# Query and key stacks of the attention layer: two heads by TensorE, six by 64 KB transfers, and one ring for the transposed weights

## The reference

```python
q, k, v = proj(Wq, bq), proj(Wk, bk), proj(Wv, bv)      # 8 heads of 32
scores = einsum('bhqd,bhkd->bhqk', q, k) * SCALE
scores = scores * (adj + adj)[:, None, :, :]
attn = softmax(scores, axis=-1)
ctx = einsum('bhqk,bhkd->bhqd', attn, v)
out = ctx @ Wo.T + bo
```

## Time and profile before

| | |
|---|---|
| median of three runs | 3148.42 us (3145.5 to 3149.03) |
| profiled execution | 3147.59 us |
| its span, first to last instruction | 3145.7 us |
| PE busy | 3023.7 us, 96% |
| DVE busy | 2083.8 us, 66% |
| ACT busy | 1724.0 us, 55% |
| POOL busy | 453.5 us, 14% |
| mean granted TensorE clock | 0.993 of full speed |
| DMA moved | 234.50 MB, mean 75 GB/s |

### The profile page before, as it was taken

How to read it: one execution, slowest core, us unless ns; L and a number is a source line. 1 busy time by engine, 2 the same in 40 slices (tenths; PEclk the granted TensorE clock), 3 DMA queues, 4 the chain that set the end, 5 groups by cost and what they waited for, 6 DMA issues and landing times.

```text
span 3145.7 us, 71077 instructions
## 1 busy us (share of the span) xinstructions
PE 3023.7 (96%) x28188; PEld 2644.0 (84%) x28188; DVE 2083.8 (66%) x4020; ACT 1724.0 (55%) x3048; POOL 453.5 (14%) x1666
## 2 busy tenths in 40 slices
PE   6999999999999999999999999999999999999999
PEld 6988789887898778987789877898778987789877
DVE  5637976379762797627975289753887438874387
ACT  3525854258552684426844278542784327853377
POOL 0101211012110122101221012111121111211112
PEclk9999999999999999999999999999999999999999
DMA  5122131121321213202133021330213302133110
GB/s 218 36 72 69 45 145 54 57 70 45 142 77 37 66 52 135 90 28 66 49 135 108 11 72 42 135 108 14 68 51 125 108 14 72 50 124 108 28 39 19
DMA packets 145271, 234.50 MB, mean 75 GB/s; under 512 B 12840, under 2 KB 113965, under 8 KB 144941
## 3 DMA queue, kind: packets, MB, share of 16 engines
q1 hardware_dynamic: 144940, 229.96, 22.5%
HBM read 120.86 MB, written 83.89 MB: 65 GB/s over the span
## 4 chain that ended last, share of the span: by engine, by line
PE 80%; DVE 10%; ACT 3%; issue 2%; SPq 2%; POOL 2%; DMA 0%; DVEq 0%; POOLq 0%; ACTq 0%
PE ps L725 15%; PE ps L497 15%; PE ps L499 14%; PE ps L498 14%; PE ps L715 9%; PE ps L743 7%; DVE rsum L1280 2%; PE ps L598 2%; SPq L400 1%; PE ps L587 1%; PE ps L756 1%; DVE ev L1379 1%; PE ps L555 1%; DVE t_lo L1210 1%; POOL rstd L461 1%
## 5 line engine op out<-in xcount | busy, mean ns | idle before, releaser
L1466 DVE CUSTOM_DVE_ANT_0 r<-ps,adjn 128x1024 f32<-128x1024 f32 x512 | 620.7, 1212 | 19.5 <-DVE xr L1502 10.3
L1141 ACT ACTIVATE r<-r,nmax 128x1024 f32<-128x1024 f32 x512 | 584.9, 1142 | 23.0 <-POOL nmax L489 22.6
L497 PE MATMUL ps<-u_hi,t_hi 128*128 128x256 f32 x2048 | 589.9, 288 | 5.8 <-DVE u_lo L1190 4.8
L499 PE MATMUL ps<-u_hi,t_lo 128*128 128x256 f32 x2048 | 579.2, 283 | 0.0
L498 PE MATMUL ps<-u_lo,t_hi 128*128 128x256 f32 x2048 | 578.8, 283 | 0.0
L725 PEld LDWEIGHTS ps<-ident,r 128*128 128x128 f32 x4096 | 462.5, 141 | 115.4 <-issue 77.6
L725 PE MATMUL ps<-ident,r 128*128 128x128 f32 x4096 | 536.7, 274 | 7.3 <-DVE pt L1482 6.9
L1482 DVE COPY pt<-ps 128x512 f32<-128x512 f32 x512 | 352.9, 689 | 92.6 <-PE ps L725 75.0
L497 PEld LDWEIGHTS ps<-u_hi,t_hi 128*128 128x128 f32 x2048 | 391.2, 191 | 14.3 <-DVE t_lo L1190 7.7
L907 ACT ACTIVATE pt<-ps 128x512 f32<-128x512 f32 x512 | 304.0, 594 | 175.8 <-PE ps L725 161.9
L498 PEld LDWEIGHTS ps<-u_lo,t_hi 128*128 128x128 f32 x2048 | 391.1, 191 | 0.0
(11 more groups left out here) (162 smaller groups left out, 5233.9 us busy)
## 6 DMA issues: line engine op xcount, KB each, us to landing
adjn<-in_adj SPq DMA_DIRECT2D x64, 512.0 KB, 3.4
t_spill<-t_hi SPq DMA_DIRECT2D x64, 512.0 KB, 4.5
t_spill<-t_lo SPq DMA_DIRECT2D x64, 512.0 KB, 5.3
t_hi<-t_spill SPq DMA_DIRECT2D x32, 1024.0 KB, 5.3
t_lo<-t_spill SPq DMA_DIRECT2D x32, 1024.0 KB, 8.0
xn<-in_x SPq DMA_DIRECT2D x16, 512.0 KB, 4.5
x_spill<-xn SPq DMA_DIRECT2D x64, 128.0 KB, 1.7
q_stack<-u_hi SPq DMA_DIRECT2D x64, 128.0 KB, 2.4
```

Of the source, the lines that this page charges most:

```text
L497: pe.matmul(dst, a_hi, b_hi, start=first, stop=False, skip_group_check=check)
L499: return pe.matmul(dst, a_lo, b_hi, start=False, stop=last, skip_group_check=check)
L1141: act.activation(r[:, s % RSLOTS, :], r[:, s % RSLOTS, :], ACT.Exp, bias=nmax[:, s % 4:s % 4 + 1], accum_out=prow[:, qt % 2, h:h + 1]).the ...
L1466: dve.tensor_tensor_reduce(out=r[:, s % RSLOTS, :], in0=ps[:, 2 * (s % 2):2 * (s % 2) + 2, :].rearrange("p a c -> p (a c)"), in1=adjn[:, q ...
```

## The change

Only heads 0 and 1 are placed by PE (`PLACED = 2`), and only their first query half and both key halves: six copies instead of 16. Everything else comes by DMA in transfers of 32 rows x 512 columns, 64 KB: for heads 2 to 7 both first halves (36) and the second key halves (18), and the second query halves of all eight heads (24), which are needed from unit 32 on. That is 78 transfers for 24. Parts are projected in another order, the first halves first, so that SP can begin when the second of the eight parts is complete; part 7 is projected behind the scores of unit 0.

The transposed weights get one ring of 15 slots for both halves, in an order that reuses the memory of the projections as their transfers complete. The single wait for all transfers becomes several: DVE and ACT wait for the first halves of heads 4 to 7 at unit 0, DVE for their second key halves at unit 2, and both for the second query halves at halves 11 to 14 of the ring, which are units 5 to 7. DVE also waits before it masks units 0 and 1, for heads 2 and 3.

```diff
-    COPIES = [(h, m, half) for half in range(HALVES) for m in range(2) for h in range(G)]
+    PLACED = 2
+    COPIES = [(h, m, half) for m, half in ((1, 0), (0, 0), (1, 1)) for h in range(PLACED)]
-    QK = [(1, 0, 0), (1, 1, 0), (0, 0, 0), (0, 1, 0), (1, 0, 1), (1, 1, 1), (0, 0, 1), (0, 1, 1)]
+    QK = [(0, 1, 0), (0, 0, 0), (1, 1, 0), (1, 0, 0), (0, 1, 1), (1, 1, 1), (0, 0, 1), (1, 0, 1)]
+        P_RING = ([(pt_0, k) for k in (2, 0, 6, 4, 3)] + [(pt_1, k) for k in range(6)] +
+                  [(pt_0, 1), (pt_0, 5), (pt_2, 0), (pt_2, 1)])
         def p_half(u, half):
+            tile, k = P_RING[(2 * u + half) % PSLOTS]
+            return tile[:, k, :, :]
...
-                for g in range(G):                       # SP: 24 transfers, 128 KB each
-                    ...
+                def moved(h, m, half, signal):           # three transfers, 64 KB each
+                    src_rows, at = slice(HD * (h % G), HD * (h % G + 1)), slice(half * 512, (half + 1) * 512)
+                    stack = (q_stack, k_stack)[m]
+                    for part, lo in enumerate((0, 0, 1) if m == 0 else (1, 0, 0)):
+                        sp.dma_start(f32(stack[HD * part:HD * (part + 1), h, at]),
+                                     f32(qk_place((h // G, m, half), lo)[src_rows, :])).then_inc(signal, 16)
+                part_done((0, 0, 0))
+                first_halves(range(PLACED, G))           # 12 transfers
+                part_done((1, 0, 0))
+                first_halves(range(G, G + 1))            # 6
+                part_done((0, 1, 1))
+                key_halves(range(PLACED, G))             # 6
+                first_halves(range(G + 1, H))            # 18
+                part_done((1, 1, 1))
+                key_halves(range(G, H))                  # 12
+                part_done((1, 0, 1))
+                for g in (1, 0):
+                    for h in range(G * g, G * (g + 1)):
+                        moved(h, 0, 1, queries_in[g])    # 24
+                wait_keys(sp, b, range(G, H))
...
+                        if u == 0:                       # ACT, before it copies half 1 of unit u
+                            wait_first(act, b, range(G, H))
+                        if 2 * u + 1 == 11:
+                            wait_queries(act, b, 1)
+                        if 2 * u + 1 == 13:
+                            wait_queries(act, b, 0)
-                        if u >= P1SLOTS:
-                            act.wait_ge(ctx_done, nth(b, 2 * NT, (u - P1SLOTS) // G + 1))
+                        if u >= 7:
+                            act.wait_ge(ctx_half, nth(b, 2 * NT, (u - 7) // G + 1))
...
+                        if u == 0:                       # DVE, before it copies half 0 of unit u
+                            wait_first(dve, b, range(G, H))
+                        if u == 2:
+                            wait_keys(dve, b, range(G, H))
+                        if 2 * u == 12:
+                            wait_queries(dve, b, 1)
+                        if 2 * u == 14:
+                            wait_queries(dve, b, 0)
```

More of the change, by code:

```diff
@@ L251, in build_program @@
         qk_hi = sem("qk_hi")
-        stacked = [sem(f"stacked{g}") for g in range(G)]
+        first_in = [sem(f"first_in{h}") for h in range(PLACED, H)]
+        keys_in = [sem(f"keys_in{h}") for h in range(PLACED, H)]
+        queries_in = [sem(f"queries_in{g}") for g in range(2)]
         copies_full = sem("copies_full")
@@ L281, in nth, with qk_place, wait_first, wait_keys @@
             return b * per + n
-        def qk_place(part, staged, kept):
+        def qk_place(part, lo):
             ft, m, half = part
-            return (staged[:, m * N + half * 512:m * N + (half + 1) * 512] if ft == 1 else
-                    kept[:, m, half * 512:(half + 1) * 512])
+            if ft == 1:
+                return (u_lo if lo else u_hi)[:, m * N + half * 512:m * N + (half + 1) * 512]
+            at = N + lo * N + half * 512 if m == 1 else 3 * N * half + lo * 512
+            return qk0[:, at:at + 512]
+        def wait_first(eng, b, heads):
+            for h in heads:
+                eng.wait_ge(first_in[h - PLACED], nth(b, 16 * 6, 16 * 6))
+        def wait_keys(eng, b, heads):
+            for h in heads:
+                eng.wait_ge(keys_in[h - PLACED], nth(b, 16 * 3, 16 * 3))
+        def wait_queries(eng, b, g):
+            eng.wait_ge(queries_in[g], nth(b, 16 * 3 * G, 16 * 3 * G))
         def copies_place(n):
@@ L388, in element @@
                     sp.dma_start(x3_d[t], xn[:, t, :]).then_inc(spilled[t // TPH], 16)
-                for g in range(G):
[L392 to L400, removed]
@@ new lines, in first_halves, with key_halves @@
+                def first_halves(heads):
+                    for h in heads:
+                        for m in range(2):
+                            moved(h, m, 0, first_in[h - PLACED])
+                def key_halves(heads):
+                    for h in heads:
+                        moved(h, 1, 1, keys_in[h - PLACED])
+                part_done = lambda part: sp.wait_ge(pr_free, nth(b, PR_UNITS, pr["qk", part] + 1))
+                part_done((0, 0, 0))
+                first_halves(range(PLACED, G))
@@ L689, in stack_copies @@
                 pe.wait_ge(pr_free, nth(b, PR_UNITS, pr["qk", (0, m, half)] + 1))
-                if 4 <= n < 3 * G or n >= 3 * G + 2:
-                    copied(b, n - (4 if n < 3 * G else 2))
-                at = slice(half * 512, (half + 1) * 512)
+                hi, lo = qk_place((0, m, half), 0), qk_place((0, m, half), 1)
                 block = lambda k, count: placer[:, (4 * h + k) * HD:(4 * h + k + count) * HD]
@@ L864, in _, with qk_part @@
                         transpose_x_half(b, 3, 0)
[L867 to L874, removed]
+                def qk_part(n):
+                    ft, m, half = QK[n]
                     pe.wait_ge(tp_free, nth(b, TP_UNITS, x_ready(3, TPH * half + TPH - 1)))
@@ L881, in _ @@
                     last.then_inc(pr_full, 1)
-                for n in range(G, 3 * G + 2):
+                qk_part(0)
+                transpose_x_late(b, 3, 1)
+                qk_part(1)
+                transpose_x_late(b, 3, 2)
+                qk_part(2)
+                qk_part(3)
+                project_pairs(b, "values", W_V, xt_wait(b, 3), range(1))
+                qk_part(4)
+                for n in range(2 * PLACED):
                     stack_copies(b, n)
+                qk_part(5)
+                for n in range(2 * PLACED, 3 * PLACED):
+                    stack_copies(b, n)
+                qk_part(6)
                 scores(b, 0)
+                qk_part(7)
                 for s in range(UNITS + 10):
```

97 lines of the change are left out of this document (49 added, 48 removed).

## The result

The changed kernel takes 3290.6 us (median of 4 runs, 3287.6 to 3293.2) against 3148.7 for the kernel before: 1.045 of its time, 95% interval 1.0438 to 1.0463. It is slower, by 142 us. The profiled execution took 3287.58 us, its span is 3285.8, its mean granted clock 0.971.

The account below looks back on a forecast made before the run. PE was taken to bound the kernel before, and SP's 78 issues to hold up the changed one. Eight elements of 16.6 + 1.5 - 0.1 us give 144 us on 3147.6: 3290 us predicted, range 3195 to 3325.

Parts of the forecast that it names:

- PE's share: Before the first scores: fewer placement matmuls bring the first mask 5.3 us earlier an element, 42 us over eight.
- The price of an issue: SP's stack transfers: 64 KB costs 0.655 us an issue, as 128 KB does; below 0.44 us the change would be faster.
- the general argument behind it: SP's other issues: 128 KB has 0.320 us, 1 MB 0.360, so half the bytes would not halve the price.
- The waits: ACT and DVE copies in units 0 to 7: transfers land late, holding the whole loop 16.6 us an element.
- unit 2's copy: DVE's copy at unit 2, awaiting the 54th transfer: at 686.9 where it stood at 677.99, 8.9 us late.
- half 1 of unit 6: ACT's copy there, awaiting the 78th transfer: at 702.6 where it stood at 685.95, 16.6 us late.
- ends just in time: Kernel before: its stream of 24 stack transfers was read as ending just in time for the ACT and DVE copies.
- The clock: After PE's idle wait: a lower granted clock costs nothing at best, 5 us at worst; 1.5 us an element taken.
- The sum: Eight elements of delay 16.6 plus clock 1.5 less 0.1 us: 144 us on 3147.6, said as 3290 us.
- The lower end of the range: The sum's own low end, 3250 us: 0.60 us an issue, no clock loss, 13 us an element.
- the cheap issue: Rival on SP's burst: 64 KB takes 0.32 to 0.37 us an issue, nobody waits, 3105 us; chance 14%.
- the in-between one: Rival on SP's burst: 0.47 to 0.60 us an issue; at 0.535, 7.3 us late, 3206 us; chance 17%.

Follow-up runs that it names:

- v3: The changed kernel with its 78 stack transfers shared by two issuing engines, 42 on SP and 36 on GpSimd: 3117.8 us, ratio 0.9905.
- x1: The changed kernel with its 42 query transfers of an element cut from 64 KB to 16 KB, keys as before: 3288.0 us, ratio 1.0448.
- x2: The kernel before with each of its 24 stack transfers of 128 KB cut in two of 64 KB: 3271.4 us, ratio 1.0402.
- x4: The changed kernel with query transfers of 128 rows x 128 columns instead of 32 rows x 512, again 64 KB: 3295.4 us, ratio 1.0471.
- x5: The changed kernel with query transfers of 32 rows x 256 columns (32 KB) read from DRAM and not from SBUF: 3236.1 us, ratio 1.0273.
- x7: The kernel before with both query parts of heads 4 to 7 complete at the fourth part and queries moved before keys: 3146.1 us, ratio 0.9987.
- x6: The changed kernel with 48 matmuls into a free part of a bank before PE waits for unit 7's second copy: 3277.8 us, ratio 1.0407.
- x8: The changed kernel with the 24 second query halves issued by GpSimd, SP keeping 54 transfers: 3221.7 us, ratio 1.0233.
- v1: The changed kernel with projections sent through DRAM in 16 stores and 21 loads, 37 issues for 78: 3165.5 us, ratio 1.0051.

## Why the prediction was right

**PE's share**: first mask 661.9, predicted 662.1. In all eight elements it comes 5.5 us earlier, for 5.3 predicted, and v3 keeps 4.1 of them.

**The price of an issue**: 0.655 us, taken from the row of the same shape. The eight bursts last 50.6 to 51.6 us, mean 50.95 / 78 = 0.653. This was the step on which the sign hung (it turned at 0.44 us). x1 and x2 show that bytes have no part in it. But the general argument behind it, that bytes are absent from all other issue times, was weaker than it looks. `t_hi`, with 0.36 us, is the first of a pair; `t_lo`, with the same 1 MB right behind it, has 0.59, and stores of 512 KB have 1.17 while the DMA engines are full (from 444 to 448 they are 102% occupied, at 405 GB/s). From the kernel before:

```profile
444.38 1.17 SPq L379 DMA_DIRECT2D t_spill<-t_lo  x1
...
543.09 0.36 SPq L385 DMA_DIRECT2D t_hi<-t_spill  x1
543.49 0.59 SPq L385 DMA_DIRECT2D t_lo<-t_spill  x1
```

An issue can thus be slowed when the engines are full, and the earlier trace rows had them at 93 to 96%. That this did not set the price of the stack transfers was shown only afterwards, by x1 and x2. Why the stack transfers are dear was seen too coarsely as well: it is not the 32 rows (x4); the source has a part in it (x5), and the rest is open.

The prediction set the Trainium skill beside this, the page DMA: Bandwidth & Descriptors. Its section Issuing engines are not separate DMA queues calls the time to initiate a transfer usually small relative to the transfer. This stream is an exception: initiating costs 0.59 us of a transfer of 2.0, and it sets the time from one transfer of the stream to the next. The section Anatomy of one DMA is about GpSimd's path, and beside the part that scales with bytes it has a fixed one of about 2.0 us; that 64 KB would cost half of 128 KB was the prediction's reading and does not follow from it. On SP the time to landing went from 2.4 us (128 KB) to 2.0 (64 KB).

**The waits**: unit 2's copy 703.25 - 16.2 = 687.05, 9.1 us late, predicted 8.9; half 1 of unit 6 at 702.0, 16.1 us late, predicted 16.6. Of the half microsecond 0.35 is in the landing: 1.45 us after the last issue's end (716.78 to 718.23) where the sum had 1.8, a value of transfers of 128 KB. The rest is in the burst. The second element is one of the latest, though. Taken the same way, half 1 of unit 6 is 14.4 to 16.2 us late in the eight elements, 15.6 in the mean; in five of them the kernel before waited for its own transfers too (x7 has the rows). That its stream "ends just in time" holds for the second element and not for these.

**The clock**: predicted 1.5 us an element, a choice between 0 and 5, so that its closeness is in part luck. From the spans, (3285.8 - 3145.7) / 8 = 17.5 us an element, less 15.6, leaves 1.9; x6 gives 1.6 to 1.7 back. The two agree within what they can tell.

**The sum**: 16.6 + 1.5 - 0.1 = 18.0 predicted, 17.5 measured. The delay was 1.0 us too large as a mean and the rest some 0.4 too small, so two small errors cancel in part. Hardly anything is made up after unit 6, as predicted. The lower end of the range was added up a little high: at 0.60 us an issue the delay is 12.4 us an element and not 13, which gives some 3246.

**The rivals**: the cheap issue falls with x1 and x2; the in-between one, for which the 0.507 at the head of a burst spoke, too: later issues are at 0.59 again, with the engines only 42 to 44% occupied. So the 0.507 is not the price that issues would have behind unoccupied engines; what it is stays open. Open as well are single slow issues, which occur in every run, of up to 1.7 us in the kernel after and 2.2 in others.

## What to carry to other kernels

Count the issues on a queue and multiply by the duration of an issue in the trace that is like yours in source, destination and shape and stands in the middle of a burst, before counting bytes: in x2, cutting each transfer in two doubled the time of the stream. Then check how full the DMA engines are, for where they are full an issue takes longer (1.17 us for 512 KB above). When work is moved from a full engine to "the DMA", the issuing engine can be the new bound; look for a second one that is idle at that time, since each pays only for its own issues (x8, v3), and lay the deadlines of every wait against the n-th issue. A wait's idle time on an engine that is not the bound (x7) is not a gain that can be had.

## What the runs showed of the hardware

An issue of these stack transfers on SP, from SBUF to SBUF, costs 0.590 us and 0.04 to the next, with 16, 64 or 128 KB (x1, before and after), and 0.601 with 128 rows for 32 (x4). From DRAM to SBUF it is 0.42 in the stream of x5, 0.32 alone, and 0.59 for 1 MB right behind another; from SBUF to DRAM 0.59 with 64 rows and 0.43 with 128 (v1). On GpSimd the same stack transfer costs 0.496 us, at the same time as SP's (x8). In the second element of the kernel after PE was idle for 5.8 us and then ran at 1.2 GHz for the first 5 us of its work; over the kernel such a stretch costs 1.6 to 1.9 us an element (x6, the spans).
